# Perceiver block on one core: Gelu of the temperature MLP by way of tanh, MLP layers and one projection at other steps

## The reference

```
scores = qk / sqrt(dk)                       # 16 heads, 64 queries, 1601 keys
feats  = [mean(scores), mean_q(max_k scores), mean_q(var_k(softmax(scores)))]      # one triple a head
hidden = gelu(feats @ w1.T + b1, approximate=False)     # 64 wide
hidden = gelu(hidden @ w2.T + b2, approximate=False)    # 64 wide
t      = exp(clip(hidden @ w3.T + b3, log 0.1, log 10))
attn   = softmax(qk / (2 t));  out = attn @ V
```

## Time and profile before

| | us |
|---|---|
| median of three runs | 1218.23 |
| lowest, highest | 1216.24, 1223.19 |
| span of the profiled execution | 1213.1 |
| TensorE matmul busy | 1101.5 (91%) |
| VectorE busy | 812.4 (67%) |
| ScalarE busy | 765.5 (63%) |
| GpSimd busy | 406.0 (33%) |

### The profile page before, as it was taken

How to read it: one execution, slowest core, us unless ns; L and a number is a source line. 1 busy time by engine, 2 the same in 40 slices (tenths; PEclk the granted TensorE clock), 3 DMA queues, 4 the chain that set the end, 5 groups by cost and what they waited for, 6 DMA issues and landing times.

```text
span 1213.1 us, 39205 instructions
## 1 busy us (share of the span) xinstructions
PE 1101.5 (91%) x14964; PEld 892.8 (74%) x14964; DVE 812.4 (67%) x2128; ACT 765.5 (63%) x1547; POOL 406.0 (33%) x420
## 2 busy tenths in 40 slices
PE   3867799999999999999999999999999999999864
PEld 3535587878888787878878797878787887867743
DVE  4467667566776776677777776577667777578245
ACT  2434576776766676767766776667767676766521
POOL 2268352223232331433232332333143233331223
PEclk9968798987979897989999898989889898989787
DMA  4610010201010111102010111102020100000000
GB/s 132 193 29 27 23 37 4 61 11 42 19 44 21 36 29 28 37 2 54 11 45 20 37 29 29 36 4 61 2 54 11 45 20 19 3 2 6 8 2 9
DMA packets 46812, 38.85 MB, mean 32 GB/s; under 512 B 14576, under 2 KB 46000, under 8 KB 46640
## 3 DMA queue, kind: packets, MB, share of 16 engines
q1 hardware_dynamic: 46640, 36.41, 11.1%
HBM read 34.30 MB, written 2.10 MB: 30 GB/s over the span
## 4 chain that ended last, share of the span: by engine, by line
PE 75%; DVE 12%; issue 5%; ACT 4%; DMA 2%; POOL 1%; SPq 1%; DVEq 0%; ACTq 0%; POOLq 0%
PE pjp L665 14%; PE s1p L704 14%; PE s2p L735 13%; PE pjp L658 12%; PE pvp L752 8%; DVE est L1392 3%; DVE negm L1386 2%; PE tlp L848 2%; PE tlp L866 1%; PE tlp L787 1%; ACT ering L1045 1%; PE tlp L842 1%; PE s2p L725 1%; PE s2p L645 1%; PE tlp L809 1%
## 5 line engine op out<-in xcount | busy, mean ns | idle before, releaser
L1386 DVE TENSOR_REDUCE negm<-s1p 128x1 f32<-128x400 f32 (+1 forms) x512 | 289.8, 566 | 199.1 <-PE s1p L704 196.6
L1045 ACT ACTIVATE ering<-s1p,negm 128x400 f32<-128x400 f32 (+1 forms) x512 | 303.8, 597 | 118.6 <-DVE negm L1386 112.2
L1056 ACT ACTIVATE pring<-s2p 128x512 f32<-128x512 f32 x427 | 240.8, 565 | 148.1 <-PE s2p L735 145.1
L704 PE MATMUL s1p<-kt,qbd 32*128 32x400 f32 (+1 forms) x1024 | 305.2, 608 | 28.1 <-ACT ering L1045 26.1
L1392 DVE BATCH_NORM_STATS2 est<-ering 128x6 f32<-128x400 f32 (+1 forms) x512 | 290.7, 568 | 19.6 <-ACT ering L1045 19.6
L735 PE MATMUL s2p<-q2bd,kt 32*128 32x128 f32 (+1 forms) x3192 | 244.6, 285 | 0.0
L735 PEld LDWEIGHTS s2p<-q2bd,kt 32*128 32x128 f32 (+1 forms) x3192 | 233.3, 194 | 5.8
L658 PE MATMUL pjp<-cr,wkv 128*128 128x256 f32 (+1 forms) x1344 | 192.4, 295 | 29.7 <-DVE vt L1358 19.2
L1264 POOL TENSOR_TENSOR cr<-stage,cr 128x512 fp32r<-128x512 f32 (+1 forms) x112 | 132.1, 1180 | 234.3 <-ACT cr L1036 234.3
L658 PEld LDWEIGHTS pjp<-cr,wkv 128*128 128x128 f32 x1344 | 171.8, 198 | 45.5 <-issue 29.1
L665 PE MATMUL pjp<-wkv,cr 128*128 128x256 f32 (+1 forms) x1200 | 195.7, 318 | 10.0 <-ACT kt L1018 9.8
(11 more groups left out here) (278 smaller groups left out, 1033.1 us busy)
## 6 DMA issues: line engine op xcount, KB each, us to landing
stage<-in_ctx SPq DMA_DIRECT2D x96, 256.0 KB, 3.0
qbd<-q_dram SPq DMA_DIRECT2D x128, 8.0 KB, 1.8
stage<-in_ctx SPq DMA_DIRECT2D x16, 65.0 KB, 2.5
vt<-in_x SPq DMA_DIRECT2D x1, 1024.0 KB, 6.8
q_dram<-late SPq DMA_DIRECT2D x1, 1024.0 KB, 4.6
late<-in_x SPq DMA_DIRECT2D x7, 128.0 KB, 2.3
out_y<-late SPq DMA_DIRECT2D x7, 128.0 KB, 1.8
late<-in_gate SPq DMA_DIRECT2D x1, 768.0 KB, 4.9
```

The lines of the kernel that those rows point to most:

```text
L704: nc.tensor.matmul(s1p[u % 3][:, 0:w], qbd[s.par][rows, g, :], kt[s.par][rows, g, lo:lo + w], start=True, stop=True).then_inc(s1_full, 1)
L1045: nc.scalar.activation(ering[:, u % 3, 0:w], s1p[u % 3][:, 0:w], ACT.Exp, bias=negm[s.par][:, p, c:c + 1]).then_inc(s1_exp, 1)
L1056: nc.scalar.activation(ring_place(s, v)[0:m, 0:n], s2_bank(s, v)[0:m, 0:n], ACT.Exp).then_inc(s2_exp, 1)
L1386: nc.vector.tensor_reduce(negm[s.par][:, p, ch:ch + 1], s1p[u % 3][:, 0:w], AX.X, ALU.max, negate=True).then_inc(s1_max, 1)
```

## The change

Each Gelu becomes 0.5 x (1 + tanh(y)) with x the biased input and y = x times a polynomial in x squared; nine VectorE instructions make y (`gelu(s, n, 0)`), ScalarE takes the tanh, and a tenth VectorE instruction (`gelu(s, n, 1)`) closes it. The intermediate q and one Horner result lie in unused columns of the bank `tlp`. All rows of the layers are 128 wide now, the upper 64 zero. The layers are at steps 5, 7 and 9, statistics 2 and 3 at 9 and 11, the temperature's exp at 10, and values of context tile 5 at step 7 in place of 9. The early exponential of the second pass goes back to its own step.

```diff
-PJ_PLAN = [(1, ("k", 4, 0)), (3, ("v", 4, 0)), (5, ("k", 5, 0)), (9, ("v", 5, 0)), (11, ("k", 6, 0)),
+PJ_PLAN = [(1, ("k", 4, 0)), (3, ("v", 4, 0)), (5, ("k", 5, 0)), (7, ("v", 5, 0)), (11, ("k", 6, 0)),
...
-S2_EARLY = S2_AT.index(STEPS + 5)
-STATS_AT = [1, 3, 8, 10]
-MLP_AT = {5: 0, 6: 1, 7: 2}
+STATS_AT = [1, 3, 9, 11]
+MLP_AT = {5: 0, 7: 1, 9: 2}
-W_AT, GELU_AT, C_AT = 2, 5, 9
+W_AT, C_AT = 2, 10
+GELU_AT = [6, 8]
+ERF_R = [7.97884216e-01, 3.63342834e-02, -3.31298998e-05, -5.52401877e-05, 3.96911353e-06, -1.33446665e-07,
+         1.80562219e-09]
+HALF_R = [2.0 * 2.0 ** k * c for k, c in enumerate(ERF_R)]
+GE_N = len(HALF_R) + 2
...
-        w1m = sb("w1m", [P, 3, DH])
+        w1m = sb("w1m", [P, 3, P])
...
         def temperature(s, n):      # TensorE
+                    if s.b == 1:
+                        pe.wait_ge(w_zero, 3)
                     for f in range(3):
-                        mm = nc.tensor.matmul(tlp[0:DH, 0:H], w1m[:, f, :], ...
+                        mm = nc.tensor.matmul(tlp[:, 0:H], w1m[:, f, :], ...
...
         def slot(s):                # TensorE, even steps: no layer here any more
-                        if step in MLP_AT and s.has(1, B):
-                            temperature(s, MLP_AT[step])
...
-            def gelu(s, n):          # ScalarE
-                need(act, mlp_full, s.lin(N_MLP, n + 1 - N_MLP))
-                nc.scalar.activation(hid[:, n, :], tlp[0:DH, 0:H], ACT.Gelu,
-                                     bias=col("b1" if n == 0 else "b2", 0, DH)).then_inc(mlp_free, 1)
+            def gelu_tanh(s, n):
+                need(act, ge, s.lin(2 * GE_N, GE_N * (n + 1) - 2 * GE_N))
+                nc.scalar.activation(tlp[:, H:2 * H], gy[:, :], ACT.Tanh).then_inc(ge_th, 1)
...
         def slot(s):                # ScalarE
-                    if s.has(1, B) and step == GELU_AT + 1:
-                        gelu(s, 1)
...
-                    if s_.has(1, B) and v < S2U and not s_.drains() and v != S2_EARLY:
+                    if s_.has(1, B) and v < S2U and not s_.drains():
                         exp2(s_, v)
...
+                    if s.has(1, B) and step in GELU_AT:
+                        gelu_tanh(s, GELU_AT.index(step))
                     s_, u = s.unit(step, 1)
                     if s_.has(0, B - 1):
                         exp1(s_, u)
...
-                    if step == GELU_AT and s.prev().has(1, B):
-                        exp2(s.prev(), S2_EARLY)
-                    if s.has(1, B) and step == GELU_AT:
-                        gelu(s, 0)
...
+            nc.gpsimd.memset(w1m[:, :, DH:P], 0.0).then_inc(w_zero, 1)      # and w2s, w3b, rows DH:P
...
+            def gelu(s, n, part):    # VectorE
+                x, b = gx[:, n, :], col("b1" if n == 0 else "b2")
+                q, low = tlp[:, H:2 * H], tlp[:, 2 * H:3 * H]
+                if part == 0:
+                    need(dve, mlp_full, s.lin(N_MLP, n + 1 - N_MLP))
+                    c = Chain(ge, s.lin(2 * GE_N, GE_N * n - 2 * GE_N))
+                    c(nc.vector.tensor_scalar(x, tlp[:, 0:H], b, 0.5, ALU.add, ALU.mult))
+                    c(nc.vector.scalar_tensor_tensor(out=q, in0=tlp[:, 0:H], scalar=b, in1=x, op0=ALU.add, op1=ALU.mult))
+                    c(nc.vector.tensor_scalar(gu[:, :], q, HALF_R[-1], HALF_R[-2], ALU.mult, ALU.add))
+                    c(nc.vector.tensor_tensor(gu[:, :], gu[:, :], q, ALU.mult))
+                    for r in HALF_R[-3:0:-1]:
+                        c(nc.vector.scalar_tensor_tensor(out=low if r == HALF_R[1] else gu[:, :], in0=gu[:, :], scalar=r,
+                                                         in1=q, op0=ALU.add, op1=ALU.mult))
+                    c(nc.vector.scalar_tensor_tensor(out=gy[:, :], in0=low, scalar=HALF_R[0], in1=x, op0=ALU.add,
+                                                     op1=ALU.mult), False)
+                else:
+                    need(dve, ge_th, s.lin(2, n + 1 - 2))
+                    nc.vector.scalar_tensor_tensor(out=hid[:, n, :], in0=q, scalar=1.0, in1=x, op0=ALU.add,
+                                                   op1=ALU.mult).then_inc(mlp_free, 1)
...
                 for step in range(STEPS):      # VectorE
+                    if s.has(1, B) and step in GELU_AT:
+                        gelu(s, GELU_AT.index(step), 0)
                     if s.has(0, B - 1):
                         maxima(s, step)
+                    if s.has(1, B) and step in GELU_AT:
+                        gelu(s, GELU_AT.index(step), 1)
                     s_, u = s.unit(step, 2)
                     if s_.has(0, B - 1):
                         sums(s_, u)
```

More of the change, by code:

```diff
@@ L345, in build @@
         hm = sb("hm", [P, DB, H])
-        hid = sb("hid", [DH, 2, H])
+        hid = sb("hid", [P, 2, H])
+        gu = sb("gu", [P, H])
+        gy = sb("gy", [P, H])
+        gx = sb("gx", [P, 2, H])
         lt = sb("lt", [P, 3, H])
@@ L429, in build @@
         mlp_full, mlp_free = sem("mlp_full"), sem("mlp_free")
+        ge, ge_th = sem("ge"), sem("ge_th")
+        w_zero = sem("w_zero")
         sc = sem("sc")
@@ L537, in _ @@
                 load_context(w, slice(0, 1))
-            for w, n in ((blockmask, "blockmask"), (w2s, "w2"), (w3b, "w3b")):
+            for w, n in ((blockmask[:, :], "blockmask"), (w2s[0:DH, :], "w2"), (w3b[0:DH, :], "w3b")):
                 sp.dma_start(w[:, :], t[n]).then_inc(consts_in, 16)
@@ L1198, in _ @@
             nc.gpsimd.memset(powh[:, :], -0.5)
+            nc.gpsimd.memset(w1m[:, :, DH:P], 0.0).then_inc(w_zero, 1)
+            pool.wait_ge(w_zero, 1)
+            nc.gpsimd.memset(w2s[DH:P, :], 0.0).then_inc(w_zero, 1)
+            pool.wait_ge(w_zero, 2)
+            nc.gpsimd.memset(w3b[DH:P, :], 0.0).then_inc(w_zero, 1)
+            pool.wait_ge(w_zero, 3)
             nc.gpsimd.memset(epst[:, :], EPS).then_inc(setup_pool, 1)
@@ L1364, in _ @@
             for f, k in enumerate((1.0 / (SQ * SK), -1.0 / SQ, 1.0 / SQ)):
[L1365 removed]
+                c(nc.vector.tensor_scalar(w1m[:, f, 0:DH], w1b[:, f, :], k, None, ALU.mult), False)
             bk = cols[:, COL["bk"][0]:COL["bk"][0] + DB]
```

8 lines of the change are left out of this document (4 added, 4 removed).

## The result

The changed kernel takes 1306.72 us (median of 4, 1301.95 to 1310.93) against 1220.71 for the kernel before, run beside it on the same chip (4 runs, 1216.24 to 1223.87): ratio 1.0706, 95% interval 1.0658 to 1.0754. Forecast was 1251, with a range that ended at 1266. The direction was right; the forecast +33.4 us is less than half of the measured 86.0.

The account below looks back on a forecast made before the run. Engine waits between scores 6 and keys 6 were taken as the only place where time can change; 5 x 1.7 + 6 x 2.9 + 4 x 1.5 + 1.5 = +33.4 us on 1218.2 gave 1251, range 1209 to 1266.

Parts of the forecast that it names:

- the rest of the slot as long as before: Sign of a right forecast: outside scores 6 to keys 6, a slot's time doesn't change.
- there nothing but its own work counts: From keys 6 to the next slot's scores 6: TensorE busy 56.09 of 56.59 us, earlier delay isn't made good.
- rivals A and B: Clock holds, 1234 us (0.18 with short layers); clock full and layers of 1.5 us, 1218 (0.12) or faster (0.18).
- Values 5's move: Step 7, ahead of scores 8: waits for the bank keys 5 uses, then takes 2.93 us at half clock.
- values 5 right after the copy-out of keys 5: Sign of a right forecast: on TensorE this projection starts once ScalarE's copy-out frees the shared bank.
- The stretch: Scores 6 to keys 6, fifteen times: +1.7 us in even slots, +2.9 in odd from the fifth batch, +1.5 in early ones.
- VectorE's chain: Nine chained operations before each tanh: 2.05 us a layer, bounds 1.5 and 2.4.
- the open question of the forecast: No row showed VectorE writing PSUM; nine operations bounded at 0.17 to 0.27 us each.
- The table loads: On ScalarE around the Gelus: they go, and with tanh for Gelu 2.7 us a slot is freed.
- The wider first layer: Six weight loads go from 64 to 128 columns: 0 to +0.3 us, taken as 0.3.
- Rival C: Statistics 3, a step earlier, meets POOL's subtraction: 0.9 us in ten of fifteen slots, +9, 1260 us; chance 0.10.
- The last slot and the end: No first-pass units to delay, but follows the MLP itself: +1.5 us, bounds 0 and 2.5.

Follow-up runs that it names:

- The short polynomial: The changed kernel with four of the nine VectorE operations of each Gelu left out; 1273.8 us, ratio 1.0450 to the kernel before.

## Why the prediction was wrong

**The step that failed** is "the rest of the slot as long as before", with its ground in the first paragraph: from keys 6 on "there nothing but its own work counts". Its own work is counted in columns, and the columns take as long as the clock allows. I had the clock in the sum only as the length of values 5, once on each side of a hole, and never asked in which state the next spell would begin. It began at half clock in every slot and stayed so up to scores 14 (0.50 to 0.52 in all fifteen windows): +35.2 us, the largest part that the sum lacked. The earlier trace rows had what was needed: values 5 at 603.61 at half clock, and a clock of 0.97 from keys 6 at 609.18 on. The question "what brought it back, and do I move that?" stood there to be asked; I asked only what a full clock would save (rivals A and B), not what more half clock would cost. No rival had it.

**Values 5's move** was treated as a matter of its bank. Alone, in the kernel before, it costs 93 us. The working put it ahead of scores 8 and behind the copy-out, which was right; the trace of after has it start at 777.26, 0.05 behind the copy-out's end, as in "values 5 right after the copy-out of keys 5".

**The stretch** was priced at +31.9 for fifteen slots and came to +38.2. Odd slot: forecast 14.9 us from scores 6 to keys 6, measured 15.07. Even slot: 13.4, measured 14.51. Up to scores 10 the even slot was even 0.5 us early (scores 10 at 783.60 are at 607.21 on the scale of before, where I had 607.7); from there to keys 6 it took 4.78 us where I had 3.2 and before 2.71, with TensorE busy all the time at a clock of 0.50.

**VectorE's chain** was sized right, though the sum given for it, 0.75 + 6 x 0.21, is 2.01 and not 2.05. ScalarE's tanh, and the chain that it waits for, in the same even slot:

```profile
775.98 0.19 ACT L1037 ACTIVATE tlp<-gy 128x16 f32<-128x16 f32 x1 [3.17 <-DVE gy L1490]
776.12 0.60 ACT L1057 ACTIVATE ering<-s1p,negm 128x400 f32<-128x400 f32 x1
776.62 0.59 ACT L1031 ACTIVATE kt<-pjp 128x512 f32<-128x512 f32 x1
```

```profile
773.98 0.23 DVE L1483 TENSOR_SCALAR gx<-tlp,cols 128x16 f32<-128x16 f32 x1 [0.99 <-PE tlp L699]
774.25 0.24 DVE L1484 SCALAR_TENSOR_TENSOR tlp<-tlp,cols,gx 128x16 f32<-128x16 f32 x1
774.53 0.17 DVE L1485 TENSOR_SCALAR gu<-tlp 128x16 f32<-128x16 f32 x1
...
775.56 0.18 DVE L1488 SCALAR_TENSOR_TENSOR tlp<-gu,tlp 128x16 f32<-128x16 f32 x1
775.77 0.17 DVE L1490 SCALAR_TENSOR_TENSOR gy<-tlp,gx 128x16 f32<-128x16 f32 x1
```

773.98 to 775.94 is 1.96 us, against 2.05 forecast. The two with a column operand start 0.27 and 0.28 before the next; the one at 775.56, which writes PSUM, starts 0.21 before the next: the open question of the forecast, what a write to PSUM costs, is answered with nothing measurable here. The short polynomial confirmed that this length is on the path. The exponential of unit 5 (776.12) comes 2.2 us after the first layer and waits for the tanh, where the forecast had 2.5.

**The table loads** went, all but one at the start, and a tanh takes 0.187 us where I had 0.22:

```profile
L1048 ACT ACT_TABLE_LOAD x1 | 1.3, 1283 | 0.7 <-PEq L1765 0.7
L1037 ACT ACTIVATE tlp<-gy 128x16 f32<-128x16 f32 x32 | 6.0, 187 | 122.0 <-DVE gy L1490 122.0
```

The row also shows where the gain went: ScalarE idles 122.0 us in front of the 32 tanhs, with the exponentials queued behind them. The run with the tanh behind the exponential took 28 us of that back.

**The wider first layer** took 0.74 to 0.81 us for six against 0.52: +0.2 to 0.3, as taken.

**Rival C** was seen in part: the scaling of the queries, at step 11 now, takes 1.48 and 1.50 us in two of its 16 executions, where the median is 0.42 and the longest before was 0.43. That is 2.1 us in all, and not 9. The part scores 14 to the next scores 6, where a wait of it would end, grew by 9.7, but by as much (11) with values 5 moved alone, so it isn't the statistics.

```profile
L1472 DVE SCALAR_TENSOR_TENSOR q2bd<-qbd,ccol x16: 417/419/1496, 145.1 to 1226.1; 128x256 f32<-128x256 f32 x16
```

**The last slot and the end** were priced at 1.5 and grew by 9.0. This part also grew by 5.0 with values 5 moved alone and by 5.5 with only matmuls added to the kernel before, and neither changes anything in the last slot's layers. No run settles the cause.

In sum: +38.2 where 31.9 was forecast, +35.2 where nothing was, +19.7 elsewhere against 1.5. That the part that was priced came out near its price is partly luck: in the even slot scores 10 was forecast 0.5 us too late and the way from there to keys 6 1.6 us too short.

## What to carry to other kernels

When dense matmuls are moved, ask what clock the work behind both places gets, not only what the moved work takes: here one projection two steps earlier, out of the light work just ahead of keys 6, cost 93 us of 1220. Compare TensorE's busy time at an equal count of matmuls first: what it rises by is the clock, and only the remainder is waiting (69.9 and 23.2 of 93.1 us here, of the first at most 4.8 for the wider layer). And put a new operation that waits for another engine behind, not ahead of, what its queue already has ready.
